# Output stages of a four-layer kernel: x and the gate loaded in pairs of chunks, six chunks ahead

## What is computed

```
xn    = norm(x)                                  # per layer: group norm, layer norm, or none
left  = proj_l(xn) * sigmoid(gate_l(xn)) (* mask)
right = proj_r(xn) * sigmoid(gate_r(xn)) (* mask)
gate  = sigmoid(xn @ Wog)
out   = einsum('bikd,bjkd->bijd', left, right)   # per channel a 256 x 256 x 256 product
out   = layernorm(out) * gate                    # layers 1 and 2: the gate is applied ahead of Wout
x     = x + out @ Wout (+ bias)                  # layers 3 and 4: the gate is applied behind Wout
```

## Time and profile before

| | us |
|---|---|
| median of three runs | 2241.92 |
| lowest and highest of them | 2240.76, 2245.84 |
| the profiled execution | 2241.74 |
| its span, first to last instruction | 2239.9 |
| PE busy | 1814.5 |
| DVE busy | 1521.0 |
| ACT busy | 1309.4 |
| POOL busy | 807.1 |
| first load of output stages 1, 2, 3, 4 issued at | 516.2, 1082.2, 1446.4, 2087.2 |
| last store of stage 3 landed, last instruction of stage 4 | about 1584, 2239.9 |

### The profile page before, as it was taken

The page is one execution under the profiler, slowest core; times in us unless marked ns, Lnnn a source line. Parts: engine busy times, 40 slices in busy tenths (PEclk is TensorE's granted clock), DMA queues, the critical chain, the costliest instruction groups (busy, mean ns, idle before and its releaser), DMA issues. The chain is left out here.

```text
span 2239.9 us, 40644 instructions
## 1 busy us (share of the span) xinstructions
PE 1814.5 (81%) x10389; PEld 966.6 (43%) x10389; DVE 1521.0 (68%) x3171; ACT 1309.4 (58%) x2413; POOL 807.1 (36%) x740
## 2 busy tenths in 40 slices
PE   0999994897998999955699786777799998499766
PEld 0333442784542344333355464633233434388432
DVE  7588885226745999966875575488488889244675
ACT  0577773466995777744599464333377776144322
POOL 0144444006960444444798000088100000000699
PEclk9999998898999999988899899899899999699999
DMA  7368677775993454547499698399547767655699
GB/s 318 111 189 256 207 240 231 283 293 199 366 335 117 154 183 159 169 142 300 155 366 361 216 305 287 158 365 399 200 127 231 238 212 224 237 230 220 210 352 338
DMA packets 353472, 542.22 MB, mean 242 GB/s; under 512 B 23627, under 2 KB 205518, under 8 KB 345686
## 3 DMA queue, kind: packets, MB, share of 16 engines
q1 hardware_dynamic: 353366, 541.01, 70.1%
HBM read 314.43 MB, written 226.49 MB: 241 GB/s over the span
## 5 line engine op out<-in xcount | busy, mean ns | idle before, releaser
L1263 POOL TENSOR_TENSOR out_scaled<-O,out_rs 128x128 f32<-128x128 f32 (+1 forms) x128 | 97.9, 767 | 739.0 <-DVE out_rs L1170 737.8
L562 PE MATMUL ps<-w_heads,hi 64*128 64x256 f16 x3072 | 292.1, 273 | 29.0 <-DVE sig L712 20.1
L1059 ACT ACTIVATE O<-ps 128x512 f32 (+1 forms) x144 | 151.8, 1054 | 233.4 <-PE ps L979 233.4
L625 ACT ACTIVATE sig<-ps,largest 128x512 f32<-128x512 f32 x384 | 246.5, 691 | 51.4 <-PE ps L562 49.9
L606 ACT ACTIVATE zs<-ps,shift 128x512 f32<-128x512 f32 x192 | 131.7, 686 | 213.3 <-PE ps L530 209.7
L1307 PE MATMUL ps<-ident,out_scaled 128*128 128x128 f32 (+1 forms) x1024 | 163.8, 285 | 107.6 <-POOL out_scaled L1263 107.5
L1307 PEld LDWEIGHTS ps<-ident,out_scaled 128*128 128x128 f32 (+1 forms) x1024 | 114.7, 134 | 278.1 <-POOL out_scaled L1263 193.7
L562 PEld LDWEIGHTS ps<-w_heads,hi 64*128 64x128 f16 x3072 | 154.3, 95 | 181.3 <-issue 65.9
L1004 DVE COPY packed<-right 128x512 f32<-128x512 f32 (+1 forms) x208 | 96.9, 490 | 190.4 <-DMA right<-left_right 141.0
L745 POOL TENSOR_TENSOR stage<-sig,mask 128x512 f32<-128x512 f32 x128 | 133.4, 1076 | 236.2 <-DVE sig L712 236.2
L979 PE MATMUL ps<-left,packed 128*128 128x256 f32 (+1 forms) x768 | 154.7, 355 | 77.8 <-DVE packed L1004 77.0
(11 more groups left out here) (136 smaller groups left out, 3645.2 us busy)
## 6 DMA issues: line engine op xcount, KB each, us to landing
left_right<-stage SPq DMA_DIRECT2D x128, 512.0 KB, 6.4
out_gs<-gate SPq DMA_DIRECT2D x256, 256.0 KB, 4.5
gate<-gates SPq DMA_DIRECT2D x96, 512.0 KB, 2.9
x_dram<-out_xo SPq DMA_DIRECT2D x192, 256.0 KB, 4.3
out_xs<-x_dram SPq DMA_DIRECT2D x192, 256.0 KB, 4.6
left<-left_right SPq DMA_DIRECT2D x22, 2048.0 KB, 7.8
right<-left_right SPq DMA_DIRECT2D x22, 2048.0 KB, 12.2
xs<-x_dram SPq DMA_DIRECT2D x64, 512.0 KB, 4.1
```

The lines of the kernel that those rows point to most:

```text
L562: last = pe.matmul(PAIR[row][:, g, kb * S:kb * S + S], tokens[half, q % 8, at:at + P], k["w_heads"][half, part, :], start=(step == 0), sto ...
L625: act.activation(sig[:, slot, :].rearrange("p (c e) -> p c e", c=4), pair(row, 0), ACT.Sigmoid, scale=k["largest"][:, 0:1]).then_inc(c["si ...
L1059: act.activation(o_of(ch), ps[h % 4 // 2][:, h % 2, :].rearrange("p (b g i) -> p b g i", b=2, g=2), ACT.Copy).then_inc(c["o_copied"].sem, 1)
```

## The change

Both inputs are loaded in pairs of chunks, 512 KB a load with 4 KB from each row. xs and gs grow from four slots to eight (`2 * PAIRS`); xo keeps four. The semaphores are one for each of four pairs. `load_pair` replaces `load_x` and `load_g`; SP calls it in every second step, for the chunks m+6 and m+7, ahead of the store of chunk m. It waits until the chunks m-2 and m-1 have left the slots. Three pairs are loaded ahead of the loop. The engines that read gs and xs index eight slots and wait for the pair's semaphore. The stores, all arithmetic and its order stay.

```diff
-    LOAD_X, LOAD_G = 4, 6 if gate_first else 5
-    RING = 4
+    LOAD = 6
+    RING, PAIRS = 4, 4
...
-        xs, gs, xo = sb("xs", [P, RING, CH]), sb("gs", [P, RING, CH]), sb("xo", [P, RING, CH])
+        xs, gs, xo = sb("xs", [P, 2 * PAIRS, CH]), sb("gs", [P, 2 * PAIRS, CH]), sb("xo", [P, RING, CH])
...
-            def load_x(i, q):
-                m = i * BODY + q
-                free = c["out_mm_done"] if gate_first else c["x_new"]
-                sp.wait_ge(free.sem, free(m - 3))
-                sp.dma_start(xs[:, q % RING, :], x[:, bass.ds(m * CH, CH)]).then_inc(c[f"xc_in{q % RING}"].sem, 16)
-
-            def load_g(i, q):
-                m = i * BODY + q
-                free = c["gated"] if gate_first else c["out_gated"]
-                sp.wait_ge(free.sem, free(m - 3))
-                sp.dma_start(gs[:, q % RING, :], gate[:, bass.ds(m * CH, CH)]).then_inc(c[f"gc_in{q % RING}"].sem, 16)
+            def load_pair(i, q):
+                m = i * BODY + q
+                slot, chunks = q // 2 % PAIRS, bass.ds(m * CH, 2 * CH)
+                free_g, free_x = (c["gated"], c["out_mm_done"]) if gate_first else (c["out_gated"], c["x_new"])
+                sp.wait_ge(free_g.sem, free_g(m - 2 * PAIRS + 2))
+                sp.dma_start(gs[:, 2 * slot:2 * slot + 2, :].rearrange("p a b -> p (a b)"), gate[:, chunks]).then_inc(c[f"gc_in{slot}"].sem, 16)
+                sp.wait_ge(free_x.sem, free_x(m - 2 * PAIRS + 2))
+                sp.dma_start(xs[:, 2 * slot:2 * slot + 2, :].rearrange("p a b -> p (a b)"), x[:, chunks]).then_inc(c[f"xc_in{slot}"].sem, 16)
 
             def step(i, q, more):
-                if more(LOAD_G):
-                    load_g(i, q + LOAD_G)
-                if more(LOAD_X):
-                    load_x(i, q + LOAD_X)
+                if q % 2 == 0 and more(LOAD):
+                    load_pair(i, q + LOAD)
                 m = i * BODY + q
                 sp.wait_ge(c["x_new"].sem, c["x_new"](m + 1))
...
-            for q in range(4):
-                load_g(0, q)
-                load_x(0, q)
-            for q in range(4, LOAD_G):
-                load_g(0, q)
+            for q in range(0, LOAD, 2):
+                load_pair(0, q)
...
-                load, stored = c[f"xc_in{q % RING}"], c[f"x_out{q % RING}"]
-                pool.wait_ge(load.sem, load(i * 64 + (q // RING + 1) * 16))
+                load, stored = c[f"xc_in{q // 2 % PAIRS}"], c[f"x_out{q % RING}"]
+                pool.wait_ge(load.sem, load(i * 32 + (q // (2 * PAIRS) + 1) * 16))
```

More of the change, by code:

```diff
@@ L1175, in gate_input @@
                 dve.wait_ge(c["wt_copied"].sem, c["wt_copied"](m + 1))
-                load = c[f"gc_in{q % RING}"]
-                dve.wait_ge(load.sem, load(i * 64 + (q // RING + 1) * 16))
+                load = c[f"gc_in{q // 2 % PAIRS}"]
+                dve.wait_ge(load.sem, load(i * 32 + (q // (2 * PAIRS) + 1) * 16))
                 dve.wait_ge(c["out_mm_done"].sem, c["out_mm_done"](m - 3))
-                dve.tensor_tensor(u[:, q % RING], TURNED[q % 4], gs[:, q % RING, :], ALU.mult).then_inc(c["gated"].sem, 1)
+                dve.tensor_tensor(u[:, q % RING], TURNED[q % 4], gs[:, q % (2 * PAIRS), :], ALU.mult).then_inc(c["gated"].sem, 1)
             def gate_output(i, q):
@@ L1183, in gate_output @@
                 dve.wait_ge(c["out_mm_done"].sem, c["out_mm_done"](m + 1))
-                load = c[f"gc_in{q % RING}"]
-                dve.wait_ge(load.sem, load(i * 64 + (q // RING + 1) * 16))
+                load = c[f"gc_in{q // 2 % PAIRS}"]
+                dve.wait_ge(load.sem, load(i * 32 + (q // (2 * PAIRS) + 1) * 16))
                 dve.wait_ge(c["x_new"].sem, c["x_new"](m - 3))
-                dve.scalar_tensor_tensor(og[:, q % RING], OUT[q % 4], k["out_bias"][:], gs[:, q % RING, :],
+                dve.scalar_tensor_tensor(og[:, q % RING], OUT[q % 4], k["out_bias"][:], gs[:, q % (2 * PAIRS), :],
                                          ALU.add, ALU.mult).then_inc(c["out_gated"].sem, 1)
@@ L1273, in add_residual @@
                     pool.wait_ge(c["counted"].sem, c["counted"](m - 3))
-                pool.tensor_tensor(xo[:, q % RING, :], og[:, q % RING], xs[:, q % RING, :], ALU.add).then_inc(c["x_new"].sem, 1)
+                pool.tensor_tensor(xo[:, q % RING, :], og[:, q % RING], xs[:, q % (2 * PAIRS), :], ALU.add).then_inc(c["x_new"].sem, 1)
             def step(i, q, more):
@@ L1318, in multiply @@
                     pe.matmul(OUT[q % 4], k["w_out"][:], u[:, q % RING], start=True, stop=False)
-                    load = c[f"xc_in{q % RING}"]
-                    pe.wait_ge(load.sem, load(i * 64 + (q // RING + 1) * 16))
-                    mm = pe.matmul(OUT[q % 4], k["ident"][:], xs[:, q % RING, :], start=False, stop=True)
+                    load = c[f"xc_in{q // 2 % PAIRS}"]
+                    pe.wait_ge(load.sem, load(i * 32 + (q // (2 * PAIRS) + 1) * 16))
+                    mm = pe.matmul(OUT[q % 4], k["ident"][:], xs[:, q % (2 * PAIRS), :], start=False, stop=True)
                 else:
@@ L1383, in output @@
     for s in range(RING):
-        for name in ("xc_in", "gc_in", "x_out"):
-            c[f"{name}{s}"].advance(16 * NCH // RING)
+        c[f"x_out{s}"].advance(16 * NCH // RING)
+    for s in range(PAIRS):
+        for name in ("xc_in", "gc_in"):
+            c[f"{name}{s}"].advance(16 * NCH // (2 * PAIRS))
     if HH < P:
```

## The result

The changed kernel is slower: 2249.38 us against 2240.76 us in the median of 19 runs each, a ratio of 1.004 with a 95% interval of 1.003 to 1.0049. One of the 19 runs of the kernel before took 5727.52 us, which the median does not feel. The forecast was 2233.4 us, the range ended at 2240. The profiled execution took 2251.64 us, with a span of 2249.8 us.

The account below looks back on a forecast made before the run. The DMA was taken to bound output stage 3, TensorE stages 1 and 2, POOL stage 4. Savings of 7.6 us in stage 3 and 1.0 in stage 4, taken as 8.5, gave 2241.9 - 8.5 = 2233.4 us; range 2229.5 to 2240.

Parts of the forecast that it names:

- What bounds the kernel: Output stages 1 and 2 bound by TensorE, 4 by POOL, 3 by the DMA at 400 GB/s, 1.97 us a chunk.
- The cost of a unit: DMA time for one 256 KB piece: 0.655 us with 2 KB rows, taken as 0.632 with 4 KB rows.
- (1): Output stages 1 and 2: nothing changes, as paired x loads land well before TensorE needs them.
- The cover: Output stages 1 and 2: six chunks of 2.15 us, about 12.9 us, before TensorE would wait for a pair of x.
- (2): Output stage 3, order on SP: each store goes out 0.7 us sooner; every second one has 0.6 us of pair ahead.
- the 6.3 us: Output stage 3: longest a store may take at 1.9 us a chunk, four chunks less the addition's 1.27 us.
- backlog: Output stage 3: DMA work already queued, up to 3.8 us said to cost nothing; taken as 2.0 us.
- (3): Output stage 3, earlier loads: 16 units of 256 KB issued before the first addition; last pair goes out at 1562.2 us.
- The fixed part: Landing time of a store beyond queue and transfer, about 1.85 us, taken from the kernel's last store.
- (5): Output stage 4: POOL stays the bound; without late x loads the last stores land in time, saving 1.0 us.
- Rival C: Stores queued behind a whole pair land 0.5 us later per four chunks: stage 3 7 us longer, 2248 us; chance 0.07.

Follow-up runs that it names:

- pairs in turn: Changed kernel with the gate pair loaded in even steps and the x pair in odd steps: 2234.09 us, ratio 0.9975 to the kernel before.

## Why the prediction was wrong, step by step

**What bounds the kernel: right, as far as the runs show.** Stage 3 was the DMA's at 2 KB rows (401 to 405 GB/s in four kernels with different rings; eight slots of xo in the kernel before change nothing), the others the engines'.

**The cost of a unit: right within some 1%.** 0.632 us for a load's and 0.655 for a store's 256 KB make 786,432 B in 1.919 us, 410 GB/s. With pairs in turn, eight slots, or both, the DMA ran at 414 to 415. The Trainium skill (DMA: Bandwidth & Descriptors, Why a DMA increments its semaphore by 16 and not by 1) has 2 KiB per partition as the least that saturates. The runs come near to that and lie a little off it: 401 to 405 GB/s with 2 KB rows, 412 to 415 with 4 KB rows in the loads, though the kernels differ in how the loads are spread and in their rings as well.

**(1) Stages 1 and 2: right**, +0.3 and 0.0 us. The cover of about 12.9 us was needed more than I said: I had the pair landing in some 5 us, it lands in 7 to 8.

**(2) The store's landing: this step failed.** SP's part was right, the store goes out 0.7 us sooner. But I added 0.6 us of the pair, 0.65 of its own and 1.85 fixed to 3.1 us, and concluded that half of the 6.3 us would be left. With the 2.0 us of backlog of (3) that makes 5.1. Measured are 7.2 us in stage 4, at 345 GB/s, and 7 in stage 3. Two terms were mis-sized. The fixed part came from the last store of the kernel, which had next to nothing behind or ahead of it: in stage 1 the first store of the changed kernel, issued at 536.51 into an empty queue, landed in 2.0 us; the first one behind a pair, issued at 541.03 and 0.8 us after the x load, in 5.7. And the pair itself lands later than its bytes say: in stage 4 a gate load of 512 KB takes 5.0 us with pairs in turn and 7.1 us in the changed kernel. A queue that serves in order and loses nothing, which is what I took, does not do this; the working has no term for single parts of a transfer that lag behind the rest.

**(3) Backlog.** I let it grow to 2.0 us at no cost. No such room existed, since the landing alone used it up; the round of four chunks closed at about 8.6 us, and the DMA moved 369 GB/s. Against the forecast's 7.6 us of gain in stage 3 stands a loss of 7.0; with the one wait removed by eight slots of xo the gain is 6.5, with pairs in turn 4.6. The forecast's sum was thus near the right size for a kernel whose additions do not wait for stores, and so was its distance of 1.88 us a chunk (1.879 with eight slots). Its parts are not borne out: the lead alone (single chunks, six ahead) gave 1.4 us in stage 3, where I had 4.9. What came on top, 3.2 us with pairs in turn and 5.1 with eight slots, mixes larger rows with loads that are spread and a ring that waits less; no run here takes these apart.

**(5) Stage 4: right in its mechanism, not for this kernel.** Where stores land in time, the stage is 1.2 to 1.3 us shorter, against 1.0 forecast. In the changed kernel it is 2.0 us longer, and its end shows it: the addition of chunk 60 waits for the store of chunk 56, which stands behind the last pair.

```profile
2240.11 1.27 POOL L1266 TENSOR_TENSOR out_xo<-out_og,out_xs 128x512 f32<-128x512 f32 x1
...
2242.36 4.92 POOL L1266 TENSOR_TENSOR out_xo<-out_og,out_xs 128x512 f32<-128x512 f32 x4 [0.98 <-DMA out<-out_xo]
```

**Rival C came true in its mechanism, and in its number partly by luck**: a store behind a whole pair, 7 us more in stage 3 and 2248 us in all, with 2249.4 measured. The point from which it decides, 6.3 us, was right as well. But its price of an even 0.5 us for each four chunks was not: between chunks 28 and 52 it was 0.88 (52.9 us for 47.6), while the first nine distances took 0.9 us less than before and those from chunk 52 on only 0.3 us more. That the sum came out at 7 us is chance. Nor were the pair and the store issued together, as C had it; the store of the round above follows the x load by 1.6 us. I gave it 0.07, on the ground that 0.6 us of a pair is less than the 1.31 us of loads of the kernel before. The evidence against that ground was in the rows: stores landed in 4.4 us in the median, when by my fixed part they should have taken 1.31 + 0.65 + 1.85 = 3.8, and the one of 1573.18 took 6. I read the difference as backlog. And the range left C out whole, where a wait that was already on the path should have kept it in.

## What to carry to other kernels

Larger loads came with some 2% more rate here, yet two of them back to back went with late landings, their own and those of the stores in their queue. Before a transfer on a critical ring is put behind larger ones, take its landing time from rows in which loads stand ahead of it, not from a lone transfer, and compare it with (slots x time of a chunk - own work); if little is left, spread the loads over the steps or give that ring more slots. Here both cured it: spreading removed most of the excess of stage 3 and cost no memory, eight slots removed the waits.

## What the runs showed of the hardware

- Where pairs of 512 KB loads issued within 0.5 us of each other follow one another with stores between, they land in 7.1 and 7.8 us; the same loads issued a step apart land in 5.0 and 5.3 us (stage 4, 345 and 354 GB/s). Cutting the rows to 2 KB does not change it (7.2 and 7.8).
- Closeness alone does not do it. At the start of the four output stages of the changed kernel the queue is empty, an x load of 512 KB follows the gate load after 0.4 us, and the gate load lands in 3.6 to 4.1 us. So what already stands in the queue has a part in it.
- The landing is late by its last parts: in stage 4 of the changed kernel the eighth of a store's 16 steps comes after 4.1 us and the last after 6.4 (3.6 and 4.4 in the kernel before). Why some parts lag behind close large loads is open.
- Near saturation the DMA moved 401 to 405 GB/s with rows of 2 KB in loads and stores, and 412 to 415 with rows of 4 KB in the loads; where the stage waited for late stores it was 364 to 390.
- With eight slots of xo in stage 3, and so with more in flight, a median store behind loads took 10.3 us at 415 GB/s and cost nothing: the time to land matters only against what the ring allows.
